# A Flamingo block with routed experts: places based by TensorE, low parts of weights on VectorE, half tiles turned

## The chip, the cores and the metric

The kernel runs on one core of one Trainium2 chip. The metric is device time of one execution in microseconds (us). The kernel before takes 543.05 us, the median of three runs (540.92 to 544.1).

## The reference, cut to what matters

```python
x = x + tanh(g_xattn) * cross_attention(layernorm(x), ctx)     # 8 x 256 tokens, 16 heads, 77 keys
xf = layernorm(x).reshape(2048, 256)
logits = xf @ router_w + router_b                               # 4 experts
top_p, top_i = top_k(softmax(logits), 2);  top_p /= sum(top_p)
h = silu(einsum('td,edf->etf', xf, w1)) * einsum('td,edf->etf', xf, w3)   # inner width 1024
x = x + tanh(g_ffn) * sum_e gates[t, e] * (h[e] @ w2[e])
```

All of it is fp32. Each token goes to two of the four experts.

## The kernel before, in words

The first block of the program (to about 187 us) is attention, batch by batch, with the routing of the first three groups of 512 tokens woven in. Routing of a group k: TensorE forms the logits, VectorE picks the two best (`choose`, line 382) and the odds (`lag`, `invert`). TensorE counts how many earlier tokens chose each expert (`rank`, line 436: products of the 0/1 choices with a triangle and with ones). ScalarE copies the counts to SBUF (`ranks_copy`, line 452). VectorE adds the running base of each expert and moves the base on (`put`, lines 458 to 464). GpSimd turns that into a row number for each token and choice (`places`, line 466) and sends the token's row there with indirect DMAs (`scatter`, line 479). `hand_out`, `rest_count` and what follows them, chains of tiny VectorE instructions, work out which expert each later tile (a "slot") has and where its rows begin.

The second block is the feed-forward part. 16 full slots of 256 rows and then 3 half slots of 128 rows are each worked through with one expert's weights, in 8 steps of 128 inner columns: 19 x 8 = 152 units u. TensorE's fp32r products are made exact enough by three terms: high x high, high x low, low x high. For each unit:

- ScalarE rounds the unit's weights of the first product to their high part (`weights_hi`, line 1398), three units ahead; GpSimd subtracts to get the low part (`weights_lo`, line 1475).
- TensorE does 12 matmuls of the first product (`up`, line 1661): weights stand, the rows of x move, 256 columns in a full slot, 128 in a half slot. The inner values come out transposed, as the second product wants them.
- ScalarE does SiLU (line 1412), VectorE the product with the gate branch (`hidden`, 1542), ScalarE its high part (`hidden_hi`, 1419), VectorE its low part (`hidden_lo`, 1547). In each even step ScalarE and VectorE also split two steps' weights of the second product (`w2_hi_of`, `w2_lo_of`, 1538).
- TensorE does the second product two units later (`down`, 1676): 3 matmuls of 256 columns for each 128 rows, so 6 in a full slot and 3 in a half slot.

Once in a slot VectorE scales the slot before (`scale`, 1556, two instructions in a full slot) at step 1 and makes the low part of the next x (`x_lo`, 1551) at step 5. TensorE turns the next x at step 5 (`turn_in`, 1650). GpSimd adds the finished rows to the output with indirect DMAs (`add_out`, 1479).

Each engine runs its queue in order, as written out by hand in its `slot` function; semaphores tie them together. Four PSUM banks `ps_gu` (NB = 4) hold the inner values of four units; weights are prepared three units ahead (AHEAD = 3). The routing of the last two groups is hung into the first 61 units by unit number (`routing(u)`). An engine learns the expert of a slot by reading it from SBUF into a register (`expert_of`, 1333, through line 1337): VectorE does that twice at the start of a slot, for the slot before and its own.

Of the kernel before, what the change touches and what calls it, by code (L numbers as in the profile page):

```python
# [16 lines left out]
P = 128  # L17
# [89 lines left out]
def flamingo_block(nc, x, ctx_t, mask, rows, columns, wq, wk, wv, wo, rw, w1, w3, w2, small_in, select_in, tokens_in, pad_in, out, grouped):  # L107

    with ExitStack() as keep:
# [54 lines left out]
        base = sb("base", [P, E])  # L164
        place = sb("place", [P, GN, E])
        ranks = sb("ranks", [P, (GN + 1) * E])
# [102 lines left out]
        rank_done, ranked, placed, based = sem("rank_done"), sem("ranked"), sem("placed"), sem("based")  # L269
# [166 lines left out]
        def rank(pe, k):  # L436
# [3 lines left out]
            if k == 0:  # L440

                pe.wait_ge(route_set, 3)
            picks = chosen_b[:].rearrange("p t e -> p (t e)")
            pe.matmul(ps_route[:, 0:GN * E], earlier[:], picks, start=True, stop=False, skip_group_check=True)
# [7 lines left out]
        def ranks_copy(act, k):  # L452
            act.wait_ge(rank_done, k + 1)

            act.wait_ge(based, k + 1)
            act.copy(ranks[:], ps_route[:, 0:(GN + 1) * E]).then_inc(ranked, 1)

        def put(dve, k):

            dve.wait_ge(ranked, k + 1)  # L460
            dve.wait_ge(based, k + 1)
            dve.tensor_tensor(place[:], ranks[:, 0:GN * E].rearrange("p (t e) -> p t e", t=GN), wide(base[:], GN), ALU.add).then_inc(placed, 1)
            dve.wait_ge(placed, k + 1)
            dve.tensor_tensor(base[:], base[:], ranks[:, GN * E:(GN + 1) * E], ALU.add).then_inc(based, 1)

        def places(pool, k):

            r = ROUTE * k
            pool.wait_ge(placed, k + 1)
            pool.wait_ge(rt_step, r + 18)  # L470
            pool.tensor_tensor(each[:], pick[:], place[:].unsqueeze(2).to_broadcast([P, GN, TOP, E]), ALU.mult).then_inc(rt_step, 1)
# [21 lines left out]
        def hand_out(dve, i):  # L493

            at = HAND * i
            dve.wait_ge(based, i + 3)
            dve.scalar_tensor_tensor(out=count[:], in0=base[:], scalar=1.0 - TILE, in1=first_row,
# [46 lines left out]
        def rest_count(dve):  # L544
            at = HAND * EARLY
            dve.wait_ge(based, NG + 1)
            for i, short in enumerate((HALF, 0)):
                dve.scalar_tensor_tensor(out=count_two[:, i], in0=base[:], scalar=-float(short), in1=first_row,
                                         op0=ALU.add, op1=ALU.subtract).then_inc(handed, 1)
# [109 lines left out]
        with nc.Block() as block:  # L659
# [161 lines left out]
            def _(pool):  # L821
# [82 lines left out]
                pool.memset(ones[:], 1.0).then_inc(route_set, 1)  # L904
                pool.tensor_copy(earlier[:], earlier_in).then_inc(route_set, 1)
# [5 lines left out]
            def _(dve):  # L911
# [83 lines left out]
                def body(b):  # L995
                    for s in range(NS):
# [23 lines left out]
                        if s == 1 and b in FINAL:  # L1020
                            invert(dve, FINAL[b])
                            put(dve, FINAL[b])
# [45 lines left out]
                dve.tensor_copy(base[:], first_row).then_inc(based, 1)  # L1068
# [248 lines left out]
        hid_lo = sb("hid_lo", [P, NB, TILE], F32R, stack=ffn)  # L1317
        y_out = sb("y_out", [P, 2, TH, D], stack=ffn)
# [7 lines left out]
        down_done, y_scaled = sem("down_done"), sem("y_scaled")  # L1326
        added = [sem(f"added{i}") for i in range(2)]
# [11 lines left out]
        def run_slots(slot):  # L1339
# [5 lines left out]
            for s in range(FULLS - 1, SLOTS):  # L1345
                slot(s, s % 2)
# [19 lines left out]
        with nc.Block() as block:  # L1366
# [30 lines left out]
            def _(act):  # L1397
# [55 lines left out]

                def routing(u):
# [16 lines left out]
                run_slots(slot)  # L1471

            @block.gpsimd
            def _(pool):
                def weights_lo(v, e, f):
                    pool.wait_ge(w_hi_done, v + 1)
                    pool.tensor_tensor(w_lo[:, f % NB], unit_weights(e, f), w_hi[:, f % NB].bitcast(F32), ALU.subtract).then_inc(w_lo_done, 1)  # L1477

# [10 lines left out]
                def slot(s):  # L1489
                    last = s == SLOTS - 1  # L1490
                    e = expert_of(pool, s)
                    for f in range(FC):
                        u = FC * s + f
                        if f == FC - AHEAD and not last:
                            e = expert_of(pool, s + 1)
# [254 lines left out]
```

## Time and profile before

| | |
|---|---|
| median of 3 runs | 543.05 us |
| the profiled execution | 542.33 us |
| its span, first to last instruction | 540.5 us |
| PE / DVE / ACT / POOL busy | 500.3 / 381.5 / 310.7 / 380.1 us |
| slots 0 to 7 (units 0 to 63) | 187.4 to 345.7 us |
| slots 8 to 15 | 345.7 to 486.0 us |
| half slots 16 to 18 and last products | 486.0 to 531.3 us |

PE is TensorE, DVE VectorE, ACT ScalarE, POOL GpSimd. The ends of matmuls are modelled, so their start-to-start distance says what one costs. Busy time is a union over overlapping instructions.

### The profile page before, as it was taken

The page shows a single profiled execution, that of the slowest core. Times are in us where ns is not written, and L with a number is a line of the kernel's source. Part 1 is how long each engine was busy: PE and PEld are TensorE (multiplying, and loading weights), DVE is VectorE, ACT ScalarE, POOL GpSimd, SP SyncE. Part 2 cuts the span into 40 slices and gives each one's busy share as a digit, 9 for nine tenths or more (in the row PEclk, how much of TensorE's full clock was granted, in tenths as well). Part 3 has the DMA queues.
Part 4 walks back from the last instruction along what each step waited for, and adds up shares of the span by engine and source line. Part 5 has one row for each costly group of instructions (what it writes and reads, how often), then busy time and mean ns, then how long its engine had stood idle before and what let it go on. Part 6 is the DMA issues. An engine that isn't in the chain of part 4 may idle for free.

```text
span 540.5 us, 11863 instructions
## 1 busy us (share of the span) xinstructions
PE 500.3 (93%) x3802; PEld 458.5 (85%) x3802; DVE 381.5 (71%) x847; ACT 310.7 (57%) x736; POOL 380.1 (70%) x341
## 2 busy tenths in 40 slices
PE   8999998989978998999989889999999999999992
PEld 6557776867767898999988889899999999999992
DVE  2588988998982388876688988766665666565661
ACT  3045457465442375786565556666777767776661
POOL 1456565469674288899777898787778777887981
PEclk9989999999977799999999999999999999999997
DMA  9999883001103100222301212311121112111101
GB/s 271 357 393 402 348 312 112 1 19 61 61 20 118 42 19 24 35 48 45 57 12 30 51 42 52 57 24 32 32 39 19 30 30 30 21 24 28 14 10 19
DMA packets 32395, 45.16 MB, mean 84 GB/s; under 512 B 9709, under 2 KB 28781, under 8 KB 32109
## 3 DMA queue, kind: packets, MB, share of 16 engines
q1 hardware_dynamic: 24807, 34.66, 18.9%
q0 software_dynamic: 6576, 8.92, 9.9%
q10 hardware_dynamic: 960, 0.94, 0.6%
q8 instruction: 26, 0.43, 0.3%
q14 instruction: 26, 0.21, 0.1%
HBM read 33.50 MB, written 21.82 MB: 102 GB/s over the span
## 4 chain that ended last, share of the span: by engine, by line
PE 44%; DVE 13%; POOL 2%; issue 2%; ACT 2%; DVEq 1%; POOLq 0%; ACTq 0%
PE ps_gu L1671 29%; PE ps_y L1688 13%; DVE w_lo L1540 3%; DVE hid_lo L1549 2%; POOL w_lo L1477 2%; DVE ps_gu L1545 2%; PE ps_x L1658 1%; ACT hid_hi L1424 1%; DVE y_out L1568 1%; DVE used_two L602 1%; DVEq L1337 1%; ACT w_hi L1410 1%; DVE total L413 1%; PE ps_y L654 1%; POOL out_x L1486 1%
## 5 line engine op out<-in xcount | busy, mean ns | idle before, releaser
L1477 POOL TENSOR_TENSOR w_lo<-w,w_hi 128x512 fp32r<-128x512 f32 x152 | 211.1, 1436 | 69.3 <-ACT w_hi L1403 68.7
L1671 PE MATMUL ps_gu<-xt_hi,w_hi 128*128 128x256 f32 (+1 forms) x608 | 172.9, 284 | 1.9 <-POOL w_lo L1477 1.5
L1671 PE MATMUL ps_gu<-xt_lo,w_hi 128*128 128x256 f32 (+1 forms) x608 | 170.5, 280 | 0.0
L1671 PE MATMUL ps_gu<-xt_hi,w_lo 128*128 128x256 f32 (+1 forms) x608 | 170.4, 280 | 0.0
L1671 PEld LDWEIGHTS ps_gu<-xt_hi,w_hi 128*128 128x128 f32 x608 | 114.8, 189 | 4.0 <-POOL w_lo L1477 3.8
L1671 PEld LDWEIGHTS ps_gu<-xt_hi,w_lo 128*128 128x128 f32 x608 | 114.8, 189 | 0.0
L1671 PEld LDWEIGHTS ps_gu<-xt_lo,w_hi 128*128 128x128 f32 x608 | 114.7, 189 | 0.0
L1403 ACT CAST w_hi<-w 128x512 fp32r x152 | 94.2, 621 | 10.2 <-issue 10.0
L1545 DVE TENSOR_TENSOR ps_gu<-act_g,ps_gu 128x256 f32<-128x256 f32 (+1 forms) x152 | 61.5, 405 | 52.3 <-ACT act_g L1417 48.8
L1417 ACT ACTIVATE act_g<-ps_gu 128x256 f32<-128x256 f32 (+1 forms) x152 | 56.2, 370 | 68.9 <-PE ps_gu L1671 67.4
L1688 PE MATMUL ps_y<-w_hi,hid_hi 128*128 128x256 f32 x280 | 81.5, 291 | 8.8 <-DVE hid_lo L1549 8.6
L1549 DVE TENSOR_TENSOR hid_lo<-ps_gu,hid_hi 128x256 fp32r<-128x256 f32 (+1 forms) x152 | 61.0, 401 | 36.8 <-ACT hid_hi L1424 36.4
L1688 PE MATMUL ps_y<-w_lo,hid_hi 128*128 128x256 f32 x280 | 79.2, 283 | 0.0
L1688 PE MATMUL ps_y<-w_hi,hid_lo 128*128 128x256 f32 x280 | 78.2, 279 | 0.0
L1424 ACT CAST hid_hi<-ps_gu 128x256 fp32r<-128x256 f32 (+1 forms) x152 | 54.2, 356 | 40.6 <-DVE ps_gu L1545 39.0
L1540 DVE TENSOR_TENSOR w_lo<-w2s,w_hi 128x512 fp32r<-128x512 f32 x76 | 68.5, 901 | 9.5 <-ACT w_hi L1410 8.5
L850 POOL TENSOR_TENSOR score<-score,lowest 128x616 f32<-128x616 f32 x32 | 38.9, 1217 | 47.5 <-DVE lowest L961 47.4
L1486 POOL DMA_INDIRECT out_x<-y_out,meta x35 | 56.9, 1626 | 9.8 <-DVE y_out L1568 4.5
L1688 PEld LDWEIGHTS ps_y<-w_hi,hid_hi 128*128 128x128 f32 x280 | 52.6, 188 | 11.4 <-DVE hid_lo L1549 11.1
L1160 PEld LDWEIGHTS ps_av<-vblock,probT 128*128 128x128 f32 (+1 forms) x320 | 41.6, 204 | 18.4 <-ACT probT L759 17.6
L1688 PEld LDWEIGHTS ps_y<-w_lo,hid_hi 128*128 128x128 f32 x280 | 52.7, 188 | 0.0
L1688 PEld LDWEIGHTS ps_y<-w_hi,hid_lo 128*128 128x128 f32 x280 | 52.6, 188 | 0.0
(198 smaller groups left out, 769.9 us busy)
## 6 DMA issues: line engine op xcount, KB each, us to landing
grouped<-in_pad SPq DMA_DIRECT2D x1, 10296.0 KB
w<-in_L_ffn_w SPq DMA_DIRECT2D x8, 1024.0 KB, 12.6
w2s<-in_L_ffn_w SPq DMA_DIRECT2D x4, 1024.0 KB, 13.7
xg<-grouped SPq DMA_DIRECT2D x16, 256.0 KB, 2.7
out_x<-xall SPq DMA_DIRECT2D x8, 256.0 KB
xall<-in_x SPq DMA_DIRECT2D x1, 1024.0 KB, 13.9
xall<-in_x SPq DMA_DIRECT2D x1, 768.0 KB, 7.7
ctxT<-in_ctx_t SPq DMA_DIRECT2D x2, 308.0 KB, 5.1
```

What stands on the lines that cost most here:

```text
L850: pool.tensor_tensor(score[:, s], score[:, s], lowest[:, s].unsqueeze(2).to_broadcast([P, HG, SK]), ALU.subtract).then_inc(lowered, 1)
L1160: mm = pe.matmul(ps_av[:].rearrange("p g h n -> p g (h n)")[:, :, HEAD0[c] * VH:HEAD0[c] * VH + w], probT[0:ROWS[c], s % 2, c, :], vblock[ ...
L1403: act.copy(w_hi[:, f % NB], unit_weights(e, f)).then_inc(w_hi_done, 1)
L1417: act.activation(act_g[:, f % 2, 0:n], ps_gu[f % NB][:, 0, 0:n], ACT.Silu).then_inc(silu_done, 1)
L1424: act.copy(hid_hi[:, f % NB, 0:n], ps_gu[f % NB][:, 1, 0:n]).then_inc(hid_hi_done, 1)
L1477: pool.tensor_tensor(w_lo[:, f % NB], unit_weights(e, f), w_hi[:, f % NB].bitcast(F32), ALU.subtract).then_inc(w_lo_done, 1)
L1486: pool.indirect_dma_start(out, bass.IndirectOffsetOnAxis(ap=meta[:, s % 2, t, E:E + 1].bitcast(U32), axis=0), y_out[:, s % 2, t, :], None, ...
L1540: dve.tensor_tensor(w2_lo[:, q % 2], pair_w2(e, q), w2_hi[:, q % 2].bitcast(F32), ALU.subtract).then_inc(w2_lo_done, 1)
L1545: dve.tensor_tensor(ps_gu[f % NB][:, 1, 0:n], act_g[:, f % 2, 0:n], ps_gu[f % NB][:, 1, 0:n], ALU.mult).then_inc(hid_done, 1)
L1549: dve.tensor_tensor(hid_lo[:, f % NB, 0:n], ps_gu[f % NB][:, 1, 0:n], hid_hi[:, f % NB, 0:n].bitcast(F32), ALU.subtract).then_inc(hid_lo_d ...
L1671: mm = pe.matmul(ps_gu[f % NB][:, m, 0:n], lhs, rhs[:, a, c, 0:n], start=(k == 0), stop=(k % (3 * DC) == 3 * DC - 1), skip_group_check=True)
L1688: mm = pe.matmul(ps_y[a][:, t], lhs, w, start=(f == 0 and t == 0 and i == 0), stop=(f == FC - 1 and i == 2), skip_group_check=True)
```

## The change

Four things. (1) `rank` starts with five tiny fp32 matmuls that add the base of each expert into the same PSUM accumulation, out of a row of ones and the old base; `ranks_copy` then yields places and new base at once, and `put` with its two VectorE instructions is gone. (2) `weights_lo` moves from GpSimd to VectorE, after `hidden_lo` of each unit (in a half slot after the product). VectorE reads the next slot's expert once more for it, at step 5. (3) In the half slots the first product has the rows of x standing and the weights moving: 6 matmuls of 256 columns. (4) Its result is not transposed; SiLU and the product give fp32 rows, TensorE transposes them (`turn_inner`), ScalarE copies them out (`inner_copy`), and the second product is a single fp32 matmul of 256 columns (`short_down`), with no splitting of inner values or of its weights.

```diff
+            for j in range(GN + 1):
+                pe.matmul(ps_route[:, j * E:(j + 1) * E], one_row[0:1, :], base[0:1, :], start=(j == 0), stop=False, skip_group_check=True)
+            pe.matmul(ps_route[:, 0:GN * E], earlier[:], picks, start=False, stop=False, skip_group_check=True)
...
         def ranks_copy(act, k):
             act.wait_ge(rank_done, k + 1)
-            act.wait_ge(based, k + 1)
-            act.copy(ranks[:], ps_route[:, 0:(GN + 1) * E]).then_inc(ranked, 1)
-        def put(dve, k):
-            dve.wait_ge(ranked, k + 1)
-            dve.wait_ge(based, k + 1)
-            dve.tensor_tensor(place[:], ranks[:, 0:GN * E].rearrange("p (t e) -> p t e", t=GN), wide(base[:], GN), ALU.add).then_inc(placed, 1)
-            dve.wait_ge(placed, k + 1)
-            dve.tensor_tensor(base[:], base[:], ranks[:, GN * E:(GN + 1) * E], ALU.add).then_inc(based, 1)
+            if k:
+                act.wait_ge(rt_step, ROUTE * k)
+            if k > 1:
+                act.wait_ge(handed, HAND * (k - 2) + 1)
+            act.copy(places_base[:], ps_route[:, 0:(GN + 1) * E]).then_inc(ranked, 1)
...
@@ VectorE, full slot
                         hidden_lo(u, f, n)
+                        if f < FC - AHEAD:
+                            weights_lo(u + AHEAD, e, f + AHEAD)
+                        elif not last:
+                            if f == FC - AHEAD:
+                                e_after = expert_of(dve, s + 1)
+                            weights_lo(u + AHEAD, e_after, f + AHEAD - FC)
@@ VectorE, half slot
+                    for f in range(FC):
+                        short_product(u, f)          # act_g = act_g * ps_gu[..., 1, 0:P]
+                        weights_lo(...)
+                        if f == 1: scale(s - 1, 1 - a, e_before)
+                        if f == 5 and not last: x_lo(s + 1, 1 - a)
@@ ScalarE, half slot
+                        silu(u, f, P)
+                        inner_copy(s, f - 1)         # inner[:, f % NB] <- ps_gu[f % NB][:, 0, 0:P]
+                        weights_hi(u + AHEAD, ...)
@@ TensorE, half slot
+                    for c in range(DC):
+                        xh, xl = (x[:, a, c, 0:P] for x in (xt_hi, xt_lo))
+                        wh, wl = (w[:, f % NB, c::DC, :] for w in (w_hi, w_lo))
+                        for i, (lhs, rhs) in enumerate(((xh, wh), (xl, wh), (xh, wl))):
+                            mm = pe.matmul(ps_gu[f % NB][:, :, 0:P], lhs, rhs, start=(c == 0 and i == 0), stop=(c == DC - 1 and i == 2))
+                def turn_inner(s, f):
+                    pe.wait_ge(hid_done, FC * s + f + 1)
+                    pe.transpose(ps_gu[f % NB][:, 0, 0:P], act_g[:, f % 2, 0:P], ident).then_inc(inner_turned, 1)
+                def short_down(s, f, a, e):
+                    pe.wait_ge(inner_copied, short_unit(s, f) + 1)
+                    pe.matmul(ps_y[a][:, 0], inner[:, f % NB], w2s[:, bass.ds(e, 1), f, :]..., start=(f == 0), stop=(f == FC - 1)).then_inc(down_done, 1)
+                    for f in range(FC):
+                        short_up(s, f, a)
+                        turn_inner(s, f - 1)
+                        short_down(s, f - 2, a, e)
```

## Rows read from the trace of the kernel before

**Rows 1.** The page's chain that ended last, by line, shares of the span.

```profile
PE ps_gu L1671 29%; PE ps_y L1688 13%; DVE w_lo L1540 3%; DVE hid_lo L1549 2%; POOL w_lo L1477 2%; DVE ps_gu L1545 2%; PE ps_x L1658 1%; ACT hid_hi L1424 1%; DVE y_out L1568 1%; DVE used_two L602 1%; DVEq L1337 1%; ACT w_hi L1410 1%; DVE total L413 1%; PE ps_y L654 1%; POOL out_x L1486 1%
```

**Rows 2.** Busy time in stretches: length, then PE, PEld, DVE, ACT, POOL, clock.

```profile
203.90:345.70 141.80, 131.12 (x1070) 127.05 (x1069) 114.85 (x244) 86.47 (x209) 119.35 (x103) 1.00 0.20 40
345.70:486.00 140.30, 140.30 (x1185) 140.30 (x1184) 88.29 (x188) 99.26 (x236) 109.12 (x81) 1.00 0.20 29
486.00:531.30 45.30, 43.77 (x378) 42.81 (x376) 27.33 (x68) 29.21 (x85) 35.83 (x27) 1.00 0.15 19
```

**Rows 3.** Chain in order of time, one full unit: start, length, what.

```profile
473.09 1.43 PE ps_gu L1671 x12
474.52 0.71 PE ps_y L1688 x6
```

**Rows 4.** Chain in order of time, one half unit.

```profile
491.96 1.29 PE ps_gu L1671 x12
493.24 0.41 PE ps_y L1688 x3
```

**Rows 5.** Waits in 187.4 to 345.7 us: total, times, longest.

```profile
PE ps_y L1688 <- DVE hid_lo L1549: 8.0, 7, 2.2
```

**Rows 6.** The page's group of the low part on GpSimd: busy, mean ns, idle before.

```profile
L1477 POOL TENSOR_TENSOR w_lo<-w,w_hi 128x512 fp32r<-128x512 f32 x152 | 211.1, 1436 | 69.3 <-ACT w_hi L1403 68.7
```

**Rows 7.** Line 1540 on VectorE: duration min/median/max in ns.

```profile
L1540 DVE TENSOR_TENSOR w_lo<-w2s,w_hi x76: 676/693/4298, 190.1 to 528.3; 128x512 fp32r<-128x512 f32 x76
```

**Rows 8.** Timeline of VectorE, back to back: start, length, instruction, idle before.

```profile
217.75 0.16 DVE L533 TENSOR_SCALAR slot_expert<-owner_no 128x4 int32<-128x4 f32 x1
...
218.50 0.42 DVE L1545 TENSOR_TENSOR ps_gu<-act_g,ps_gu 128x256 f32<-128x256 f32 x1
218.83 0.69 DVE L1540 TENSOR_TENSOR w_lo<-w2s,w_hi 128x512 fp32r<-128x512 f32 x1
219.43 0.42 DVE L1549 TENSOR_TENSOR hid_lo<-ps_gu,hid_hi 128x256 fp32r<-128x256 f32 x1
219.77 0.42 DVE L1545 TENSOR_TENSOR ps_gu<-act_g,ps_gu 128x256 f32<-128x256 f32 x1
```

**Rows 9.** Timeline of VectorE over the start of a slot.

```profile
451.87 0.42 DVE L1549 TENSOR_TENSOR hid_lo<-ps_gu,hid_hi 128x256 fp32r<-128x256 f32 x1 [0.44 <-ACT hid_hi L1424]
453.32 0.43 DVE L1545 TENSOR_TENSOR ps_gu<-act_g,ps_gu 128x256 f32<-128x256 f32 x1 [1.03 <-ACT act_g L1417]
```

**Rows 10.** Timeline of VectorE, the pair that scales.

```profile
456.49 0.86 DVE L1568 TENSOR_SCALAR y_out<-ps_y,meta 128x256 f32<-128x256 f32 x2
```

**Rows 11.** Timelines of GpSimd and VectorE at one tiny VectorE instruction.

```profile
282.69 3.10 POOL L1477 TENSOR_TENSOR w_lo<-w,w_hi 128x512 fp32r<-128x512 f32 x2
...
282.72 3.11 DVE L413 TENSOR_SCALAR total<-behind 128x4 f32<-128x4 f32 x1
```

**Rows 12.** Line 462, the first instruction of `put`: min/median/max ns.

```profile
L462 DVE TENSOR_TENSOR place<-ranks,base x4: 982/1122/1209, 114.5 to 278.0; 128x16 f32<-128x16 f32 x4
```

**Rows 13.** TensorE's routing groups in 187.4 to 345.7 us: busy, mean ns.

```profile
L349 PE MATMUL ps_route<-rws,ctxT 128*128 128x64 f32 x16 | 1.9, 272 | 0.0
L448 PE MATMUL ps_route<-chosen_b,ones 128*128 128x4 bf16 x8 | 0.5, 164 | 0.0
```

**Rows 14.** Timeline of TensorE, fp32 matmuls of 256 columns and transposes.

```profile
56.91 1.46 PE L1182 MATMUL ps_misc<-wos,ctxnT 128*128 128x256 f32 x6
...
463.93 0.60 PE L1658 MATMUL ps_x<-small,xg 128*128 128x128 f32 x4
```

**Rows 15.** Timeline of ScalarE in a half slot.

```profile
527.37 0.28 ACT L1417 ACTIVATE act_g<-ps_gu 128x128 f32<-128x128 f32 x1 [0.80 <-PE ps_gu L1671]
527.55 0.61 ACT L1410 CAST w_hi<-w2s 128x512 fp32r x1
528.05 0.27 ACT L1424 CAST hid_hi<-ps_gu 128x128 fp32r<-128x128 f32 x1
```

**Rows 16.** The half slots' VectorE product, shapes apart: busy, mean ns.

```profile
L1545 DVE TENSOR_TENSOR ps_gu<-act_g,ps_gu 128x128 f32<-128x128 f32 x24 | 7.1, 296 | 8.7 <-ACT act_g L1417 8.1 <-issue 0.4
```

More of the change, by code:

```diff
@@ L1344, in run_slots @@
                     slot(2 * j + UNROLLED + i, (UNROLLED + i) % 2)
-            for s in range(FULLS - 1, SLOTS):
-                slot(s, s % 2)
+            slot(FULLS - 1, (FULLS - 1) % 2)
+            for s in range(FULLS, SLOTS):
+                short(s, s % 2)
         def tiles_of(s):
@@ L1592, in slot, with short_product, short @@
                             routing(u)
+                def short_product(u, f):
+                    dve.wait_ge(silu_done, u + 1)
+                    dve.tensor_tensor(act_g[:, f % 2, 0:P], act_g[:, f % 2, 0:P], ps_gu[f % NB][:, 1, 0:P], ALU.mult).then_inc(hid_done, 1)
+                def short(s, a):
+                    last = s == SLOTS - 1
+                    e_before = expert_of(dve, s - 1)
+                    e = expert_of(dve, s)
+                    for f in range(FC):
+                        u = FC * s + f
+                        short_product(u, f)
+                        if f < FC - AHEAD:
+                            weights_lo(u + AHEAD, e, f + AHEAD)
+                        elif not last:
+                            if f == FC - AHEAD:
+                                e_after = expert_of(dve, s + 1)
+                            weights_lo(u + AHEAD, e_after, f + AHEAD - FC)
+                        if f == 1:
+                            scale(s - 1, 1 - a, e_before)
+                        if f == 5 and not last:
+                            x_lo(s + 1, 1 - a)
                 def routing(u):
@@ L1609, in routing @@
                         lag(dve, k)
-                    if u in (3, 36):
-                        put(dve, k)
                     if u in (4, 38):
@@ L1643, in _ @@
                 slot.engine = dve
+                e = expert_of(dve, 0)
+                weights_lo(0, e, 0)
                 x_lo(0, 0)
-                run_slots(slot)
+                for f in range(1, AHEAD):
+                    weights_lo(f, e, f)
+                run_slots(slot, short)
                 scale(SLOTS - 1, (SLOTS - 1) % 2, expert_of(dve, SLOTS - 1))
@@ new lines, in turn_inner @@
+                def turn_inner(s, f):
[3 more added lines that the diff above has]
+                    pe.wait_ge(inner_copied, short_unit(s, f) + 1)
+                    if f == 0:
+                        pe.wait_ge(y_scaled, tiles_before(s - 1))
+                    pe.matmul(ps_y[a][:, 0], inner[:, f % NB], w2s[:, bass.ds(e, 1), f, :].rearrange("p o n -> p (o n)"),
+                              start=(f == 0), stop=(f == FC - 1)).then_inc(down_done, 1)
@@ new lines, in short @@
+                def short(s, a):
+                    pe.wait_ge(x_lo_done, s + 1)
+                    e = expert_of(pe, s)
+                    if s > FULLS:
+                        e_before = expert_of(pe, s - 1)
+                    for f in range(FC):
+                        short_up(s, f, a)
+                        if f:
+                            turn_inner(s, f - 1)
+                        elif s > FULLS:
+                            turn_inner(s - 1, FC - 1)
+                        if f >= 2:
+                            short_down(s, f - 2, a, e)
+                        elif s > FULLS:
+                            short_down(s - 1, FC - 2 + f, 1 - a, e_before)
+                        else:
+                            down(s - 1, FC - 2 + f, 1 - a)
+                        if f == 5 and s < SLOTS - 1:
+                            turn_in(s + 1, 1 - a)
+                    if s == SLOTS - 1:
+                        short_down(s, FC - 2, a, e)
+                        turn_inner(s, FC - 1)
+                        short_down(s, FC - 1, a, e)
@@ L1719, in _ @@
                 fill_gap(pe, FILL["split"], ps_y[1][:, 0])
-                run_slots(slot)
-                for f in (FC - 2, FC - 1):
-                    down(SLOTS - 1, f, (SLOTS - 1) % 2)
+                run_slots(slot, short)
         ffn.close()
```

88 lines of the change are left out of this document (59 added, 29 removed).

## Prediction

> **What bounds the kernel now.** I read the page's chain first, then the busy times by stretch, then the waits, then the timelines of VectorE and TensorE. The chain is mostly TensorE's two products [rows 1], and the reader should see that the rest of it are small shares of VectorE and GpSimd steps. The stretches say where those sit [rows 2]. In 345.7 to 486.0 us TensorE is busy all 140.30 us: there only fewer or shorter matmuls help. In 203.9 to 345.7 us, where routing is hung in, it is busy 131.12 of 141.80, and 8.0 us of the rest are waits of the second product for the low part of the inner values, on VectorE [rows 5]. In the half slots it is busy 43.77 of 45.30.
>
> A full unit is 1.43 + 0.71 = 2.14 us of TensorE [rows 3]: 18 matmuls at 0.119. Four transposes a slot cost about 0.11 each (0.60 less one duration of 0.27, over three [rows 14]), so a full slot is 8 x 2.14 + 0.43 = 17.55 us, and eight of them are the 140.3. A half unit is 1.29 + 0.41 = 1.70 us [rows 4]: its 12 matmuls of 128 columns cost 0.108 each, nearly what 256 columns cost.
>
> **Half slots.** Before, 45.3 us. TensorE's new unit: 6 matmuls of 256 columns x 0.119 = 0.71; one transpose 0.11; one fp32 matmul of 256 columns, which six in a row price at (1.46 - 0.38)/5 = 0.216 (0.38 is the length of the last) [rows 14]. Sum 1.04 instead of 1.70, so 24 units want 25 us, with turned x and the end 26.5.
>
> The Trainium skill, "FP8 and Floating Point Precision", TensorE Precision Notes, says that true fp32 takes four passes through the array. From the rows fp32r's 256 columns cost 0.119 and fp32's 0.216, not four times; by four times 0.119 the unit would be 1.30 and the half slots 5 to 6 us longer than by the rows. The row decides for the sum; the rule stays as a rival.
>
> The other engines: ScalarE's starts are 0.18 after a 128-column SiLU and 0.50 after a weight cast [rows 15], the copy taken as the SiLU: 0.86 a unit. VectorE: product 0.30 [rows 16] less the 0.09 by which back-to-back instructions overlap (0.42 long, 0.33 apart [rows 8]) = 0.21, low part of the weights 0.60 (218.83 to 219.43 [rows 8]): 0.81. Both fit under 1.04, but with little room, and now TensorE's transpose of unit f - 1 waits directly for VectorE's product, one unit behind. VectorE stops to read experts at each slot's start: 451.87 to 453.32 us, 1.45 between starts [rows 9], 0.85 more than the 0.60 of the instruction that it now stands behind; and it reads once more at step 5, half of that reading and the wait, about 0.8 instead of 0.34, so 0.45 more. With scale (0.39) and half an x_lo (0.34) VectorE has 8 x 0.81 + 2.0 = 8.5 us a slot, as much as TensorE (8.3 + 0.2), and a stall at each of the two places reaches TensorE since the slack is under one unit. I take 1.8 us a slot for that: 10.3 for slots 17 and 18, 12 for slot 16 (last full-size second products, two scales), and 1.5 for the end: 34. Bounds: 26.5 (TensorE alone) and 37. **Saved: 11.3**, 8 to 18.
>
> **Full slots in steady state.** VectorE's queue gets the low parts. Price: the same shape from w2 has a median of 0.693 us [rows 7], 0.60 to the next start [rows 8]; the stretched ones (up to 4.3) go below. On GpSimd it was 1.44 [rows 6]. Even unit, back to back: 0.33 product + 0.60 w2 + 0.34 low inner part + 0.60 = 1.87. Odd unit: the low part waits for ScalarE's cast, 0.44 of idle after a product of 0.43 [rows 9]: 0.87 + 0.34 + 0.60 = 1.81. Four of each are 14.7; two scales 0.78 (0.86 for the pair, [rows 10]), x_lo 0.61, expert reads 0.85 + 0.45. Sum **17.4 us a slot against TensorE's 17.55**. It just fits. TensorE has about one unit of slack, so the bunched reads do not reach it while the sums hold; I add 0.2 a slot for the places where they do: 7 unrolled or looped slots, **+1.4 us**. Below: 0. Above: if nothing overlapped (each instruction its full length) VectorE would need 19.6, +2 a slot.
>
> **Full slots with routing, slots 1 to 7.** Today 141.8. TensorE's own work is 7 x 17.55 = 122.9, plus 16 products x 0.12 and 8 transposes x 0.11 and some tiny ones [rows 13, 14]: 126. What goes: the stretching of VectorE by GpSimd. A four-column instruction took 3.11 us while two of GpSimd's low parts ran [rows 11]; its neighbours take 0.16. With GpSimd's 1.44 us instructions gone, nothing holds them. What comes: VectorE now has no room, so its routing instructions stand on the path. I count 83 of them between units 4 and 60; six in a row take 218.50 - 217.75 = 0.75 [rows 8], 0.125 each, ones that depend on the last about 0.20, so 0.17 on average: 14 us. VectorE: 7 x 17.4 + 14 = 136. The matmuls of `rank` at unit 34 come right behind the choice of unit 33, which VectorE now makes later; the stall of 1 to 2 us falls in slot 4, which has little else, and is inside the sum. So 136.3 instead of 141.8: **-5.5**, bounds -13 (TensorE's sum with half of the routing hidden) and +2 (0.2 for each instruction and some bunching).
>
> **Start and attention.** `put` goes: two VectorE instructions, the first 1.12 us at the median (held by GpSimd) [rows 12], the second a tiny one; two of the four stand in attention, where VectorE is nearly as full as TensorE: at most 2.6. Five tiny matmuls come to each `rank`: between the 0.06 of a bf16 4-column one (0.5 us for 8) and the 0.12 of an fp32 64-column one (1.9 for 16) [rows 13], 0.3 to 0.6 each time. I take **-1.0**, bounds -2.6 and +1. The ready chain of slot 0 is unchanged: the low part for unit 0 is made by VectorE in 0.7 before x_lo, where GpSimd took 1.3. ScalarE's new waits in `ranks_copy` (places of the group before, `hand_out` of two before) are for things done many units earlier; behind them stand SiLU and casts, which thus lose nothing. GpSimd's scatters are no longer spaced by low parts and go earlier; nothing waits for them.
>
> **Sum.** -11.3 + 1.4 - 5.5 - 1.0 = -16.4 on the profiled execution of 542.33 (span 540.5): 525.9. The runs' median is 0.7 above the profiled one: 526.5.
>
> **Rivals.**
> - *VectorE is mildly the bound.* If VectorE's loop is 18.3 us a slot, not 17.4 (overlap of 0.05 instead of 0.09, a little more for reads), slots 8 to 15 cost 0.75 x 8 = 6 more and the routed ones gain nothing: 525.9 - 1.4 + 6 + 5.5 + 1 = 537. For: the margin of 0.15. Against: the start-to-start distances are measured.
> - *VectorE decides all full slots, slower.* One mechanism: the low part of the weights stands between `hidden_lo` and the next product in VectorE's queue, and that product releases ScalarE and then the next low part. It decides from 18.65 us a slot, where 16 x 1.1 us eat what half slots and attention bring plus the 5.5; at 19.6 (no overlap) it is 16 x 2.05 = 33 more in place of 1.4 and -5.5, less 12.3: 563. Near the threshold, 545 to 550. Against: it needs every overlap of [rows 8] to fail.
> - *Fp32 second product by the passes rule.* TensorE's half unit is 1.30: TensorE then hides VectorE's stalls partly, half slots 37 to 39, total 530. Against: the row of six.
> - *Everything hidden.* VectorE's routing falls into TensorE's slack and the half slots come near 28 us: 514.
> - *The gain in the half slots does not come.* If transposing and copying make a round trip of two units on each unit, a unit is no shorter than 1.6: 535. Against: two units lie between product and use.
>
> **How the numbers follow.** Forecast 0.57; mild bound 0.19; slower 0.09; passes 0.04; everything hidden 0.07; no gain in half slots 0.04. A change of 0.5% is 2.7 us, about what can be told. Slower gets 0.09; same 0.05 (the high end of the mild bound); faster 0.86. The range reaches from the hidden case's side, 515, to the mild bound's top, 540. The likeliest case alone: 520 to 532.
>
> **What would show it.** Slots 8 to 15 keep 17.5 to 17.8 us and TensorE 97% or more busy there; if VectorE is the bound, the waits show TensorE's second product waiting for line `hidden_lo`, each slot, and slots over 18. No tiny VectorE instruction over 0.3 us after 190 us. The weights' low part on VectorE has 0.69 us. In half slots matmuls of 256 columns stand 0.119 apart, the fp32 one takes 0.22 of TensorE, and waits of the transpose for the product appear near a slot's start and step 5. The forecast is wrong if slots 8 to 15 sum to over 144 or the half slots to over 38.

## The result

The changed kernel takes 537.86 us (median of 16 runs, 532.46 to 540.99) against 542.17 (16 runs, 540.91 to 544.1): a ratio of 0.9901, 95% interval 0.9877 to 0.9925. It is faster by 1%: 4.3 us by the medians, 5.4 by the ratio. The two differ because three of the 16 runs (540.59 to 540.99), more than 1.5% above the fastest, are counted as slow and left out of the ratio; the median of the other 13 is 536.8. The forecast was 526.5: right in direction, but wrong in size, since 16.4 us were forecast and a third of that came. The measured time still lies inside the stated range of 515 to 540, near its slow end. The spread of the runs has grown from 3.2 to 8.5 us. The profiled execution has a span of 538.6 us, 1.9 below the one before, so it is one of the slower executions; what follows compares stages, each with the same stage before.

The page's chain, by engine and by line, answers to [rows 1]:

```profile
PE 29%; DVE 22%; issue 6%; ACT 4%; DVEq 2%; ACTq 0%; POOL 0%
PE ps_gu L1728 15%; PE ps_y L1745 7%; DVE w_lo L1567 7%; DVE ps_gu L1572 4%; DVE w_lo L1563 4%; DVE hid_lo L1576 3%; PE ps_gu L1774 2%; ACT hid_hi L1430 2%; DVEq L1338 2%; PE ps_y L1785 2%; DVE y_out L1595 2%; DVE xt_lo L1581 1%; ACT w_hi L1416 1%; PE ps_gu L1779 1%; PE ps_route L448 1%
```

VectorE has taken a good part of TensorE's share of the chain, and a tiny thing, `ps_route` L448 (the base matmuls of `rank`), has 1%. The stretches, columns as in [rows 2], for slots 1 to 7, 8 to 15 and the half slots:

```profile
210.00:351.10 141.10, 135.03 (x1086) 131.52 (x1085) 113.58 (x300) 88.28 (x212) 45.84 (x43) 0.98 0.22 43
351.10:491.50 140.40, 140.37 (x1179) 139.91 (x1179) 116.03 (x250) 97.24 (x233) 24.80 (x16) 1.00 0.19 28
491.50:529.30 37.80, 34.09 (x231) 30.05 (x229) 23.38 (x55) 23.03 (x73) 7.47 (x4) 1.00 0.13 16
```

Slots 8 to 15 are as they were, with TensorE full. Slots 1 to 7 have lost only 0.7 us, with a mean clock of 0.98 instead of 1.00. The half slots went from 45.3 to 37.8. And the feed-forward part begins later.

The table reads each profile by the start of the first SiLU of a slot (half slots: to the last SiLU; "end" from there to the end of the span; one execution each). The first rows are before and after, the others are the experiments below; "single reads" and "choice at 32" each stand on the base in one matmul, "experts kept" on the single reads.

| us | first SiLU | before it at half clock | slots 0-7 | slots 8-15 | half slots | end | span |
|---|---|---|---|---|---|---|---|
| before | 189.1 | 23.9 | 158.8 | 139.6 | 41.8 | 11.2 | 540.5 |
| changed | 193.6 | 30.7 | 159.2 | 140.1 | 34.0 | 11.6 | 538.6 |
| base on VectorE | 190.2 | 27.3 | 155.9 | 139.5 | 33.9 | 11.8 | 531.3 |
| base part alone | 190.0 | 20.5 | 165.1 | 139.6 | 43.3 | 11.2 | 549.1 |
| base early | 191.2 | 27.3 | 156.5 | 140.0 | 34.1 | 11.9 | 533.7 |
| rank late | 196.0 | 34.1 | 155.3 | 140.1 | 34.0 | 11.8 | 537.3 |
| low parts alone | 186.6 | 17.1 | 155.8 | 139.5 | 40.1 | 11.2 | 533.2 |
| half slots alone | 189.0 | 23.9 | 158.7 | 139.1 | 36.5 | 11.9 | 535.2 |
| narrow second product | 185.0 | 13.7 | 156.0 | 139.5 | 33.7 | 11.7 | 525.9 |
| base in one matmul | 186.5 | 20.5 | 155.5 | 140.1 | 34.1 | 11.9 | 528.2 |
| + single reads on TensorE | 184.8 | 13.7 | 155.5 | 140.1 | 32.6 | 11.9 | 525.0 |
| + choice at 32 | 187.4 | 23.9 | 153.2 | 140.1 | 34.1 | 11.9 | 526.8 |
| + experts kept | 188.8 | 23.9 | 150.3 | 138.8 | 31.6 | 11.7 | 521.2 |
| + kept and choice at 32 | 182.0 | 10.2 | 149.5 | 138.7 | 31.7 | 11.9 | 513.7 |

The second column is the time before the first SiLU in which TensorE's granted clock was 0.5 (1.2 GHz, its lower level) instead of 1.0. It differs much from execution to execution, and with it the first SiLU: less half of that column, all 14 first SiLUs lie between 175 and 180 us. So the first column alone says little of a kernel.

**The rank.** TensorE's timeline of the changed kernel at unit 34, start, length, then what and, in brackets, the idle time before it:

```profile
274.83 0.28 PE L1745 MATMUL ps_y<-w_hi,hid_lo 128*128 128x256 f32 x1
277.69 2.29 PE L448 MATMUL ps_route<-places_base,one_row 1*128 1x4 f32 x10 [2.58 <-DVE chosen_b L390]
279.91 0.19 PE L449 MATMUL ps_route<-chosen_b,earlier 128*128 128x16 bf16 x1
...
280.50 0.41 PE L1728 MATMUL ps_gu<-xt_lo,w_hi 128*128 128x256 f32 x1
280.72 0.41 PE L1728 MATMUL ps_gu<-xt_hi,w_lo 128*128 128x256 f32 x1
```

Three things cost here. TensorE stood idle for 2.58 us, waiting for VectorE's choice. Five fp32 matmuls are ten records (the expectations call them passes), and they took 2.2 us. And the product behind them goes at 0.213 us a matmul instead of 0.119: the granted clock is at its lower level, from 277.5 us on. That is inside the wait, 0.2 us ahead of the ten records. In attention there is no such wait (the matmuls stood idle for 0.3 us at most ahead of its two ranks), and the clock falls all the same, 0.4 us behind the first rank. Stretches with their clock in the third column from the end:

```profile
100.00:110.20 10.20, 10.13 (x79) 8.47 (x79) 9.09 (x22) 4.43 (x10) 4.35 (x4) 1.00 0.01 2
110.20:113.60 3.40, 3.40 (x12) 2.71 (x10) 2.26 (x5) 0.00 (x0) 1.22 (x1) 0.50 0.00 0
277.50:284.30 6.80, 6.61 (x37) 6.59 (x38) 2.43 (x6) 1.58 (x5) 1.20 (x1) 0.50 0.16 19
```

In the changed kernel a half-clock stretch stands at three of the four ranks (3.4, 3.4 and 6.8 us long), in the kernel before at none. With 0.213 us a matmul for 0.119, a half-clock stretch in which TensorE is the bound loses 0.44 of its length: an estimate of 6 us together.

### The profile page after: what moved, and what is told of

It reads as the page before. It is cut to its first block, busy times and chain, and to the rows that moved or that the text cites. A ratio compares the mean times of both kernels' runs of the same rounds, so it can differ in the third digit from the quotient of the medians.

```text
span 538.6 us, 11563 instructions
## 1 busy us (share of the span) xinstructions
PE 500.7 (93%) x3698; PEld 454.5 (84%) x3698; DVE 405.2 (75%) x955; ACT 305.1 (57%) x724; POOL 182.7 (34%) x190
## 3 DMA queue, kind: packets, MB, share of 16 engines
q1 hardware_dynamic: 24807, 34.66, 18.9%
## 4 chain that ended last, share of the span: by engine, by line
PE 29%; DVE 22%; issue 6%; ACT 4%; DVEq 2%; ACTq 0%; POOL 0%
PE ps_gu L1728 15%; PE ps_y L1745 7%; DVE w_lo L1567 7%; DVE ps_gu L1572 4%; DVE w_lo L1563 4%; DVE hid_lo L1576 3%; PE ps_gu L1774 2%; ACT hid_hi L1430 2%; DVEq L1338 2%; PE ps_y L1785 2%; DVE y_out L1595 2%; DVE xt_lo L1581 1%; ACT w_hi L1416 1%; PE ps_gu L1779 1%; PE ps_route L448 1%
## 5 line engine op out<-in xcount | busy, mean ns | idle before, releaser
L1728 PE MATMUL ps_gu<-xt_hi,w_hi 128*128 128x256 f32 x512 | 147.2, 287 | 0.3 <-DVE xt_lo L1581 0.2
L1728 PE MATMUL ps_gu<-xt_lo,w_hi 128*128 128x256 f32 x512 | 144.7, 283 | 0.0
L1728 PE MATMUL ps_gu<-xt_hi,w_lo 128*128 128x256 f32 x512 | 144.4, 282 | 0.0
L1567 DVE TENSOR_TENSOR w_lo<-w,w_hi 128x512 fp32r<-128x512 f32 x152 | 104.0, 685 | 17.0 <-ACT w_hi L1409 10.0
L1728 PEld LDWEIGHTS ps_gu<-xt_lo,w_hi 128*128 128x128 f32 x512 | 96.9, 189 | 0.0
L1728 PEld LDWEIGHTS ps_gu<-xt_hi,w_lo 128*128 128x128 f32 x512 | 96.9, 189 | 0.0
L1430 ACT CAST hid_hi<-ps_gu 128x256 fp32r<-128x256 f32 x128 | 47.8, 373 | 75.3 <-DVE ps_gu L1572 72.0
L1576 DVE TENSOR_TENSOR hid_lo<-ps_gu,hid_hi 128x256 fp32r<-128x256 f32 x128 | 54.0, 422 | 28.6 <-ACT hid_hi L1430 27.3
L1572 DVE TENSOR_TENSOR ps_gu<-act_g,ps_gu 128x256 f32<-128x256 f32 x128 | 54.1, 423 | 18.1 <-issue 10.4
L1159 PE MATMUL ps_av<-vblock,probT 128*128 128x102 f32 (+2 forms) x320 | 43.8, 286 | 8.8 <-ACT probT L758 7.4
## 6 DMA issues: line engine op xcount, KB each, us to landing
w2s<-in_L_ffn_w SPq DMA_DIRECT2D x4, 1024.0 KB, 13.7
ctxT<-in_ctx_t SPq DMA_DIRECT2D x2, 308.0 KB, 5.1
```

What stands on the lines that cost most here:

```text
L1159: mm = pe.matmul(ps_av[:].rearrange("p g h n -> p g (h n)")[:, :, HEAD0[c] * VH:HEAD0[c] * VH + w], probT[0:ROWS[c], s % 2, c, :], vblock[ ...
L1430: act.copy(hid_hi[:, f % NB, 0:n], ps_gu[f % NB][:, 1, 0:n]).then_inc(hid_hi_done, 1)
L1567: dve.tensor_tensor(w_lo[:, f % NB], unit_weights(e, f), w_hi[:, f % NB].bitcast(F32), ALU.subtract).then_inc(w_lo_done, 1)
L1572: dve.tensor_tensor(ps_gu[f % NB][:, 1, 0:n], act_g[:, f % 2, 0:n], ps_gu[f % NB][:, 1, 0:n], ALU.mult).then_inc(hid_done, 1)
L1576: dve.tensor_tensor(hid_lo[:, f % NB, 0:n], ps_gu[f % NB][:, 1, 0:n], hid_hi[:, f % NB, 0:n].bitcast(F32), ALU.subtract).then_inc(hid_lo_d ...
L1728: mm = pe.matmul(ps_gu[f % NB][:, m, 0:n], lhs, rhs[:, a, c, 0:n], start=(k == 0), stop=(k % (3 * DC) == 3 * DC - 1), skip_group_check=True)
```

## The experiments

Each is compared with runs of the kernel before on the same chip; ratios are those of its runs to these.

**Base on VectorE.** The first part of the change undone: `put`, `place`, `base` and `ranks` as before, everything else changed.

```diff
-            for j in range(GN + 1):
-                pe.matmul(ps_route[:, j * E:(j + 1) * E], one_row[0:1, :], base[0:1, :], ...)
+            dve.tensor_tensor(place[:], ranks[:, 0:GN * E].rearrange("p (t e) -> p t e", t=GN), wide(base[:], GN), ALU.add).then_inc(placed, 1)
+            dve.tensor_tensor(base[:], base[:], ranks[:, GN * E:(GN + 1) * E], ALU.add).then_inc(based, 1)
```

> The changed kernel with its first part undone: the base is again added by VectorE (put), rank has no fp32 matmuls. Theory A (TensorE's base costs: ten fp32 passes of 0.112 us a rank, four ranks, make 4.5 us, and a lower granted clock follows the rank three times, some 1.7 us in attention twice and 3.4 in slot 4): this kernel takes about 529 us, 8 to 9 less than the changed kernel's 537.9, and no half clock follows a rank in attention. Rival B (low parts on VectorE cost it, and the later start of the feed-forward part is chance): it stays at 536 to 539, or gets worse by the 1.1 us stretches of put.

532.5 us, ratio 0.9831 (0.9799 to 0.9863). By the ratios the change is worth 9.2 us without its first part and 5.4 with it. The half clock no longer follows a rank in attention (142 to 149 us, around its second one):

```profile
142.00:149.00 7.00, 6.32 (x49) 5.29 (x50) 6.76 (x16) 1.53 (x4) 5.46 (x5) 1.00 0.12 41
274.70:278.10 3.40, 3.40 (x18) 3.40 (x17) 1.76 (x5) 1.33 (x4) 0.02 (x1) 0.51 0.34 39
```

In slot 4 it still does, for 3.4 us instead of 6.8. There the wait is the changed kernel's 2.58 us and the ten records are gone, so the wait alone is enough for a half clock. Theory A's direction holds, with 3.8 us by the ratios (5.4 by the medians) instead of 8 to 9. In the profiles 3.3 of it are in slots 0 to 7 (two ranks).

**The base part alone.** The same lines, added to the kernel before.

> The kernel before with the first part of the change alone. Theory A: 4.5 us of fp32 passes and one or two clock drops in attention: 547 to 549 against 542.2. Rival B: within 1 us of before, since the tiny matmuls fall into TensorE's waits and put goes.

554.3 us, ratio 1.0221 (1.0181 to 1.026): 12 us slower, more than either theory gave. Its profile has half-clock stretches at 144.2, 219.3, 277.3 and 308.0 us, 3.4 us each, that the kernel before has not:

```profile
144.20:147.60 3.40, 3.40 (x10) 2.59 (x10) 2.04 (x6) 0.14 (x1) 2.70 (x3) 0.50 0.22 80
219.30:222.70 3.40, 3.40 (x18) 3.40 (x18) 2.38 (x10) 1.97 (x5) 2.33 (x2) 0.50 0.36 43
277.30:280.70 3.40, 3.40 (x18) 3.40 (x17) 1.95 (x6) 1.33 (x4) 1.70 (x2) 0.50 0.00 0
308.00:311.40 3.40, 3.40 (x19) 3.40 (x18) 2.95 (x9) 2.72 (x7) 1.77 (x2) 0.51 0.36 39
```

So slots 0 to 7 take 165.1 us, 6.3 more: two ranks' records are 2.2, three half-clock stretches some 4.5 (an estimate, by the 0.44 above). Two of the four stand behind a rank. The other two stand behind waits of TensorE for `hidden_lo` of 2.0 and 2.2 us. The kernel before has the same two waits (at 214.7 and 300.0 us) and kept its clock, so such a wait is followed by half clock in one execution and not in another. The runs (550.3 to 554.4) say that other executions were worse than this one; the section on the clock over all runs splits the 12 us.

**Base early.** The wait for the choice moved behind the base's matmuls.

```diff
-            pe.wait_ge(rt_step, ROUTE * k + 7)
             pe.wait_ge(lg_copied, k + 1)
...
+            pe.wait_ge(rt_step, ROUTE * k + 7)
             pe.matmul(ps_route[:, 0:GN * E], earlier[:], picks, start=False, ...)
```

> The changed kernel, with the base's fp32 matmuls issued before the wait for VectorE's choice instead of after it. Theory A with the passes themselves as its main term: they fall into the idle time ahead of each rank (6.0 us over four in the changed kernel's trace, 2.6 of it at slot 4): 4 us less than the changed kernel, 534. If the lower clock is what costs, and it comes from TensorE's idle time before the rank, it goes too: 531. Rival B: no difference.

534.79 us, ratio 0.9854 (0.9817 to 0.9891): 2.5 us by the ratios below the changed kernel, whose interval it overlaps, so not surely told apart. In slot 4 the records now fall into the wait, and the slot takes 22.3 us instead of 25.0. There is nothing to gain at the other ranks: the 6.0 us of idle time in the expectation count the weight loads' wait beside the matmuls' (2.58 us in slot 4, 0.3 at most elsewhere). The half clock at the two attention ranks (108.5 and 146.0 us) stayed, with no wait in front of them.

**Rank late.**

```diff
-                    if u == 34:
+                    if u == 36:
                         rank(pe, NG - 1)
-                    if u in (2, 35):
+                    if u in (2, 37):
                         ranks_copy(act, NG - 2 if u == 2 else k)
```

> The changed kernel with the last group's rank two units later on TensorE (unit 36, its copy at 37), so that VectorE's choice is ready. Theory: slot 4 loses its 2.6 us of idle time and the half clock behind it (25.0 us becomes 20): 5 us less than the changed kernel, 533. Rival: VectorE sets slot 4 anyway, the stall only moves to the next unit: no more than 1 us less.

535.62 us, ratio 0.9883 (0.9844 to 0.9922), which overlaps the changed kernel's interval: not told apart by the times. By the profile slot 4 went from 25.0 to 21.4 us, so the stall is real. The half clock behind it did not go, as the theory wanted: with no wait left, 3.4 us of it (284.5 to 287.9) begin 1.1 us behind the ten records. That execution lost the gain again in attention (first SiLU at 196.0, with 34.1 us at half clock before it).

**Low parts alone**: base on VectorE and the half slots as before.

```diff
             for s in range(FULLS, SLOTS):
-                short(s, s % 2)
+                slot(s, s % 2)
```

> The second part of the change alone: low parts of the weights on VectorE, base by VectorE, half slots as before. Theory A (low parts bring only the contention with GpSimd back, about 3 us in slots 0 to 7, and nothing in 8 to 15): 539.5, slots 0 to 7 at 156, half slots at 41 to 42 by the SiLUs. Rival B (VectorE, near full, costs as much as it saves): 542 or more, slots 8 to 15 over 140.5.

536.88 us, ratio 0.9914 (0.9896 to 0.9932), 4.7 us and more than theory A's 2.7. Slots 0 to 7 are 155.8 as it said, slots 8 to 15 139.5: the low parts cost nothing there. The half slots gain 1.7 us too, which it did not have.

**Half slots alone**: base on VectorE, the low parts on GpSimd everywhere.

```diff
+                def weights_lo(v, e, f):     # under gpsimd, called as before; the VectorE one gone
+                    pool.wait_ge(w_hi_done, v + 1)
+                    pool.tensor_tensor(w_lo[:, f % NB], ...)
```

> The half slots of the change alone: low parts stay on GpSimd in all slots, base by VectorE. Theory A (TensorE's new half unit of 1.25 us, with the fp32 product at 0.43, is just matched by GpSimd's 1.24 to 1.29 a low part): half slots 35, kernel 535. Rival B (GpSimd becomes the bound in half slots, and the gain needs the low parts on VectorE): half slots over 38, kernel 538 or more.

536.58 us, ratio 0.9909 (0.9888 to 0.993), half slots 36.5 us. Between the theories: GpSimd now does hold TensorE in the half slots, for 4.9 us (waits of 485.8 to 524 us):

```profile
PE ps_gu L1774 <- POOL w_lo L1514: 4.9, 4, 1.3
```

The two parts add up: 0.9914 x 0.9909 = 0.9824, and with the base on VectorE both together gave 0.9831.

**Narrow second product**, on the kernel with its base on VectorE. In six of eight steps the fp32 product of the half slots covers 128 of 256 output columns; the other columns miss those terms.

```diff
+                    n = D if f in (0, FC - 1) else D // 2
-                    pe.matmul(ps_y[a][:, 0], inner[:, f % NB], w2s[:, bass.ds(e, 1), f, :]...,
+                    pe.matmul(ps_y[a][:, 0, 0:n], inner[:, f % NB], w2s[:, bass.ds(e, 1), f, 0:n]...,
```

> The changed kernel with the base by VectorE, and in the half slots the fp32 second product of 6 of 8 steps only half as wide (128 of 256 columns; the other half of the output rows is left out there). Theory A (the fp32 product takes 2 passes of 0.215 us and TensorE sets the half unit): 18 x 0.215 = 3.9 us less than with base by VectorE alone (532.5), so 528.7. Rival B (the round trip through ScalarE, VectorE and the expert reads sets the half slots): under 1 us less.

529.79 us, ratio 0.9799 (0.9774 to 0.9824), which overlaps that of the base on VectorE (0.9831), and the profile does not put the gain in the half slots: 33.7 us against 33.9. A half-clock stretch of 3.4 us (504.1 to 507.5) fell into them, which hides up to 1.5, and the attention part was 5.2 us shorter in this execution. So at most 1.6 of the 3.9 us are there: inconclusive, between the two. The second product's price is thus not shown by taking it away; it rests on the timeline in the next section.

**Base in one matmul**, ahead of the wait.

```diff
-            for j in range(GN + 1):
-                pe.matmul(ps_route[:, j * E:(j + 1) * E], one_row[0:1, :], base[0:1, :], start=(j == 0), ...)
+            pe.matmul(ps_route[:, 0:(GN + 1) * E].rearrange("p (t e) -> p t e", e=E), one_row[0:1, :],
+                      wide(base[0:1, :], GN + 1), start=True, stop=False, skip_group_check=True)
```

> The changed kernel, the base added by one fp32 matmul of 20 columns (a repeated row) instead of five of 4, ahead of the wait for the choice. Theory A (each fp32 pass of a one-row product costs 0.112 us whatever its columns, so 2 passes in place of 10): 0.9 us a rank less, and fewer clock drops behind the rank in attention: 531.5, as good as the base on VectorE (532.5) or better. Rival B (the clock drops come from the place of the rank, not from its length): as base early, 534.8.

530.03 us, ratio 0.979 (0.9766 to 0.9815); base early had 0.9854 (0.9817 to 0.9891). Against base early only the number of records differs, and the intervals just miss each other. No half clock follows the attention ranks: the stretch behind the first, and TensorE's rank at unit 34:

```profile
107.00:113.60 6.60, 6.28 (x47) 4.69 (x47) 6.23 (x20) 3.13 (x8) 2.71 (x4) 1.00 0.12 40
```

```profile
267.07 0.39 PE L446 MATMUL ps_route<-places_base,one_row 1*128 1x20 f32 x2
269.74 0.18 PE L448 MATMUL ps_route<-chosen_b,earlier 128*128 128x16 bf16 x1 [2.27 <-DVE chosen_b L390]
```

Two records instead of ten; the stall of 2.27 us for the choice remains, and so does a half clock of 3.4 us behind it. TensorE's base is then no worse than VectorE's.

**Single reads on TensorE**, on top of it.

```diff
+                    if s == FULLS:
+                        known.update({i: expert_of(pe, i) for i in range(FULLS, SLOTS)})
                     pe.wait_ge(x_lo_done, s + 1)
-                    e = expert_of(pe, s)
-                    if s > FULLS:
-                        e_before = expert_of(pe, s - 1)
+                    e, e_before = known[s], known.get(s - 1)
```

> The kernel with the base in one matmul (530.0 us), and TensorE reads the experts of all three half slots once, at the start of the first, instead of two reads at each of slots 17 and 18 and one at 16. Theory A (each read holds TensorE's queue for 0.5 us with the array idle): the border units of slots 17 and 18 go from 2.8 to 1.8 us, slots 17 and 18 lose 1 us each: 528. Rival B (the border waits for VectorE's low part and x, the reads are hidden behind it): no difference, 530.

529.8 us, ratio 0.9784 (0.9755 to 0.9814): the times do not separate it. The profiles do. In the kernel with its base on VectorE, whose half slots are the same, TensorE's sequencer reads an expert five times, and the first matmul of slot 17 waits for nothing else that the profile shows:

```profile
L1339 PEldq TENSOR_LOAD <-slot_expert x5: 296/309/487, 482.8 to 508.5; - x5
```

```profile
496.04 0.62 PE L1788 MATMUL ps_y<-w2s,inner 128*128 x2
497.42 0.36 PE L1777 MATMUL ps_gu<-w_hi,xt_hi 128*128 128x256 f32 x1 [0.75 <-issue]
```

With single reads the same border, from second product to the first matmul of slot 17, is 0.28 us instead of 1.38:

```profile
490.82 0.62 PE L1784 MATMUL ps_y<-w2s,inner 128*128 x2
491.10 0.47 PE L1773 MATMUL ps_gu<-w_hi,xt_hi 128*128 128x256 f32 x1
```

and the half slots take 32.6 instead of 34.1 us.

**Choice at 32**, on the base in one matmul.

```diff
-                    if u == 33:
+                    if u == 32:
                         choose(dve, k)
```

> The kernel with the base in one matmul, VectorE's choice of the last group hung into unit 32 instead of 33, so that TensorE's rank at unit 34 does not wait. Theory A (the stall and the half clock behind it are what makes slot 4 22 to 25 us): slot 4 at 20, no half clock around 270 us, kernel 528. Rival B (VectorE's queue sets slot 4; the same instructions only stand elsewhere): slot 4 within 0.5 us of 22.3.

528.83 us, ratio 0.9745 (0.9711 to 0.9779), which overlaps that of the base in one matmul. By the profile theory A holds: slot 4 is 19.9 us instead of 22.3, and from 260 to 285 us the clock is full and TensorE busy throughout:

```profile
260.00:285.00 25.00, 25.00 (x215) 24.69 (x214) 20.72 (x56) 15.85 (x40) 7.12 (x11) 1.00 0.16 26
```

**Experts kept.** Single reads on TensorE, and VectorE keeps what it has read.

```diff
+                    if isinstance(s, int) and s in known:
+                        e_before, e = known.get(s - 1), known[s]
+                    elif (not isinstance(s, int)) and a != UNROLLED % 2:
+                        e_before, e = known["here"], known["after"]
+                    else:
...
-                                e_after = expert_of(dve, s + 1)
+                                e_after = known["after"] = expert_of(dve, s + 1)   # and known[s + 1]
```

> As the single reads on TensorE, and VectorE keeps the experts that it has read in registers too: one read in a slot instead of three. Theory A (VectorE sets slots 1 to 7 and the starts of half slots, and a slot's reads cost it 0.85 us at the start): slots 0 to 7 at 152, half slots 31.5, kernel 524. Rival B (the reads run ahead of VectorE's engine and cost nothing): as the single reads, slots 0 to 7 at 155.5.

522.63 us, ratio 0.9639 (0.9607 to 0.9671): 7 us better than single reads alone. VectorE's 57 reads are 28:

```profile
L1337 DVEq TENSOR_LOAD <-slot_expert x28: 300/308/689, 183.9 to 496.1; - x28
```

Slots 0 to 7 go from 155.5 to 150.3, slots 8 to 15 from 140.1 to 138.8, half slots from 32.6 to 31.6. Rival B falls. Of the 5.2 us in slots 0 to 7, 2.7 are in slot 4: VectorE is earlier there, TensorE waits 1.24 us instead of 2.27, and no half clock follows.

**Experts kept, choice at 32.**

> Both: experts kept in registers, and the choice at unit 32. If both theories hold, 522; if VectorE's reads cost nothing, 528 or more.

518.97 us, ratio 0.9583 (0.9534 to 0.9633), the lowest of all and below the 522 of both theories: 4.2% below before, about 17 us below the change as it was made by these ratios. From experts kept alone (0.9639) it is not told apart. The profiled execution, at 515.58, is one of its faster ones.

**The clock over all runs.** For every run the span and the mean granted clock are on record. Their product is about the time that the run would have taken at full clock with TensorE as the bound throughout, and the rest of the span is what the half clock cost at most (estimates; means over the runs that enter the ratios):

| us | runs | span x clock | span x (1 - clock) |
|---|---|---|---|
| before, with the first four experiments | 9 | 525.1 | 14.5 |
| before, with the next four | 11 | 525.3 | 14.5 |
| before, with the last four | 11 | 525.3 | 14.9 |
| changed | 13 | 516.0 | 19.0 |
| base on VectorE | 6 | 513.0 | 17.6 |
| base part alone | 6 | 530.6 | 20.5 |
| base early | 6 | 514.9 | 16.7 |
| rank late | 6 | 514.7 | 18.9 |
| low parts alone | 6 | 519.3 | 15.4 |
| half slots alone | 6 | 520.2 | 14.6 |
| narrow second product | 6 | 511.8 | 16.4 |
| base in one matmul | 6 | 513.0 | 15.2 |
| single reads on TensorE | 7 | 512.1 | 15.6 |
| choice at 32 | 6 | 512.4 | 14.0 |
| experts kept | 6 | 506.2 | 14.5 |
| experts kept, choice at 32 | 6 | 504.5 | 12.4 |

The change took some 9 us of work away and brought 4 to 5 us of half clock, against the kernel before as it ran beside the experiments. The first part of it cost 3.0 us of work and 1.4 of clock against the base on VectorE, the ten records 3.0 and 3.8 against the base in one matmul. The base part alone cost 5.5 and 6.0 us: its 12 us are as much clock as work. Why both are larger there than within the full change stays open. The changed kernel's 16 spans lie 8.2 us apart, their products with the clock 3.1 us: most of the spread of its runs is the clock.

## Why the prediction was wrong

By the ratios 11.0 of the 16.4 us are missing. Two steps failed. The base matmuls and their clock were put at nearly nothing, and the part that they belong to made the kernel 3.8 us slower where 1.0 us of gain was forecast (4.8 us). And the fp32 second product was priced at half of its cost, which the half slots show (3.8 us). Both prices come from one mistake: the time from one record to the next was taken for the time of a matmul, and an fp32 matmul has two records (a transpose has one). The slots below are read from the table, one execution each; the terms are the prediction's own.

- **Start and attention, -1.0 forecast, +4.5 in the profile: a step that failed.** I priced the five base matmuls at 0.06 to 0.12 each from rows of 4 and 64 columns. They are fp32 and have two records each, ten in all, 0.112 us apart at full clock with their 4 columns: 1.1 us a rank, twice the upper bound. (The row of 64 columns was misread too: its 16 records are 8 matmuls.) I gave the term no clock. A half clock follows the ranks in attention in all three profiles with ten records in the full change (changed kernel, base early, rank late; six ranks), behind one of the two in the base part alone, and in none of the ten profiles with two or no such records (20 ranks). Undoing that part alone was worth 3.8 us by the ratios. The +4.5 itself is partly chance: the changed kernel's execution had 10.2 us of half clock at its start (28.3 to 38.5 us), ahead of any rank, the one before 3.4, and 6.8 us less at the end of attention.
- **Slots 1 to 7, -5.5 forecast, 0.7 measured.** The mechanism was right: before, 30 VectorE instructions between 188 and 350 us took over 0.72 us (up to 4.3); with the base on VectorE two did (0.74 at most). Slots 0 to 7 then gain 2.9 of the 5.5. The rest of the miss stands in slot 4: the wait at unit 34 was foreseen at 1 to 2 us and called inside the sum; it was 2.58, with the ten records and 6.8 us of half clock at it. Choice at 32 shows it: 2.4 us off slot 4 for one moved number.
- **Steady slots, +1.4 forecast, +0.6 measured.** The low part took 0.68 us, forecast 0.69, and VectorE just fits. With the base on VectorE, these slots take what they took before (139.5 in three profiles with the low parts on VectorE); the 0.6 more comes with the base on TensorE (140.0 to 140.1 in six profiles), though no routing stands here, and is not explained. Experts kept brought 1.3 us even here, so VectorE sits at the edge as the 17.4 against 17.55 said:

```profile
L1567 DVE TENSOR_TENSOR w_lo<-w,w_hi x152: 678/682/737, 190.5 to 524.0; 128x512 fp32r<-128x512 f32 x152
```

- **Half slots, -11.3 forecast, -7.5 measured: the other step that failed.** A mis-read row: I took the six records of [rows 14] for six matmuls. They are three. The program issues four such matmuls a batch, 32 in eight batches, and the trace before has 64 records of that line:

```profile
L1182 PE MATMUL ps_misc<-wos,ctxnT x64: 379/379/635, 56.6 to 181.9; 128*128 128x256 f32 x64
```

  So an fp32 matmul of 256 columns costs 0.43 us, not 0.216, and the half unit 1.25 instead of 1.04, 5.0 us over 24 units. The timeline in the changed kernel (510.79 to 512.04, a whole unit):

```profile
510.79 0.27 PE L1779 MATMUL ps_gu<-small,act_g 128*128 128x128 f32 x1
510.90 0.60 PE L1785 MATMUL ps_y<-w2s,inner 128*128 x2
511.15 0.47 PE L1774 MATMUL ps_gu<-w_hi,xt_hi 128*128 128x256 f32 x1
...
512.04 0.27 PE L1779 MATMUL ps_gu<-small,act_g 128*128 128x128 f32 x1
```

  The rival built on the four passes rule (the Trainium skill, "FP8 and Floating Point Precision", TensorE Precision Notes) was right about its term: 37 to 39 us for the half slots, 37.8 measured. The trace agrees with the rule when one counts records against the program: 0.43 is 3.6 times 0.119. It had a chance of 0.04. The other thing missed here: TensorE's own reads of the expert, new in `short`, 1.5 us in all by the profiles. I had seen such reads on VectorE and not looked for them in the added TensorE code. Whether 1.8 us a slot for VectorE's reads and stalls was right no run shows by itself; experts kept took 1.0 us off the three half slots together.

Adding up the profile's stages: +4.5 +0.4 +0.6 -7.8 +0.4 = -1.9. The slower rivals (VectorE as the bound) did not happen: the time of 537 that the mild one gave came about, but by other costs. That the measured time is inside the range is luck, since the range was built for that rival.

## What to carry to other kernels

Before taking a duration from a group, count its records against the matmuls that the program issues; fp32 ones come in pairs here. Price a tiny instruction by its records, not by its columns, and see what TensorE's clock does at a wait and at a run of near-empty matmuls: the stretch after it can cost more than both. Set span times clock beside the span of every run before a difference of a few us is explained. When an engine becomes nearly full, its register reads are work; a value that stays valid is best read once.

## What the runs showed of the hardware

- An fp32 matmul with one row and 4 columns is two records, 0.112 us apart at full clock and 0.213 at half (changed kernel). With 20 columns the two are as far apart, 0.133, as the first two of a rank with 4 columns, 0.132.
- An fp32 matmul of 128 rows and 256 columns is two records 0.216 us apart; an fp32r one is one record, 0.119 from the next.
- In attention the half clock came behind seven of eight ranks with ten such records and behind none of ten with two. In slot 4 it came with every wait of 2.27 to 2.59 us (six profiles), and behind ten records without a wait (rank late). With waits of 2.0 to 2.2 us for `hidden_lo` it came in the base part alone and not in the kernel before or with the half slots alone.
- The other half-clock stretches (start, end of attention) move between executions: the first SiLU lies between 182.0 and 196.0 us over kernels whose attention parts hardly differ.
- A read of an integer from SBUF into a register holds an engine's queue for about 0.5 us (load 0.31, two register steps 0.15 to 0.19 and 0.02), on TensorE too (the rows of line 1338).
- With GpSimd free of element-wise work, VectorE's low parts of the weights kept their length to within 0.06 us (0.678 to 0.737), although GpSimd still issued all indirect DMAs; the same shape had gone up to 4.3 in the kernel before.
